# A fused transformer layer: f32 scores, in-PSUM exponentials and DMA transposes instead of split f16 scores and PE transposes

## What is computed

```python
q = (x @ Wq).reshape(B, N, HEADS, DIM_HEAD).transpose(0, 2, 1, 3)      # x: layernorm of x
k = (context @ Wk).reshape(B, M, HEADS, DIM_HEAD).transpose(0, 2, 1, 3)
v = (context @ Wv).reshape(B, M, HEADS, DIM_HEAD).transpose(0, 2, 1, 3)
dots = jnp.einsum('bhnd,bhmd->bhnm', q, k) * SCALE
attn = jax.nn.softmax(dots, axis=-1)
out = jnp.einsum('bhnm,bhmd->bhnd', attn, v)
out = out.transpose(0, 2, 1, 3).reshape(B, N, HEADS * DIM_HEAD)
return out @ Wo + bo
```

## Time and profile before

| | |
|---|---|
| median of 3 runs | 1029.28 us (1024.49 to 1030.27) |
| the profiled execution's own time | 1028.92 us |
| its span, first to last instruction | 1027.0 us |
| PE, DVE, POOL, ACT busy | 870.6, 831.1, 774.3, 684.0 us |
| PE weight loads (PEld, beside PE) | 720.6 us |
| mean granted TensorE clock | 0.935 of full speed |

### The profile page before, as it was taken

How to read it: one execution, slowest core, us unless ns; L and a number is a source line. 1 busy time by engine, 2 the same in 40 slices (tenths; PEclk the granted TensorE clock), 3 DMA queues, 4 the chain that set the end, 5 groups by cost and what they waited for, 6 DMA issues and landing times.

```text
span 1027.0 us, 29818 instructions
## 1 busy us (share of the span) xinstructions
PE 870.6 (85%) x8554; PEld 720.6 (70%) x8554; DVE 831.1 (81%) x2343; ACT 684.0 (67%) x2029; POOL 774.3 (75%) x1237
## 2 busy tenths in 40 slices
PE   7989998999999999999999999999998461049895
PEld 7777786878787887878787887887776261036664
DVE  5899888989999989899999999998988657025563
ACT  3777776778777778778777777777775113037774
POOL 5788888898989898888889898989886503735554
PEclk9999999999999999999999999999999655559998
DMA  9111111111111111111111211111100840111120
GB/s 233 33 33 33 32 33 33 33 33 36 49 42 32 31 31 31 31 31 31 31 31 32 59 33 31 31 31 31 31 2 2 129 162 14 52 43 53 47 54 17
DMA packets 56836, 45.11 MB, mean 44 GB/s; under 512 B 8367, under 2 KB 54578, under 8 KB 56769
## 3 DMA queue, kind: packets, MB, share of 16 engines
q1 hardware_dynamic: 54464, 40.01, 15.9%
q0 software_dynamic: 2304, 4.25, 1.3%
HBM read 37.25 MB, written 7.52 MB: 44 GB/s over the span
## 4 chain that ended last, share of the span: by engine, by line
PE 36%; POOL 31%; issue 13%; DVE 12%; ACT 4%; DMA 1%; POOLq 1%; DVEq 1%; ACTq 0%; SPq 0%
POOL Pn L925 10%; PE bank L396 6%; PE bank L373 6%; PE bank L420 4%; POOL cT L916 4%; PE bank L1369 3%; PE bank L413 3%; PE bank L385 3%; POOL sorted_rows L1232 3%; POOL chi L906 2%; PE bank L1384 2%; DVE cs L839 2%; DVE nmax L783 2%; POOL clo L910 2%; DVE Tl L777 1%
## 5 line engine op out<-in xcount | busy, mean ns | idle before, releaser
L925 POOL TENSOR_TENSOR Pn<-Pe,rsum 128x1028 f32<-128x1028 f32 x128 | 243.1, 1899 | 74.4 <-DVE rsum L798 74.4
L713 ACT ACTIVATE Pe<-bank,nmax 128x257 f32<-128x257 f32 x512 | 240.5, 475 | 30.1 <-DVE nmax L783 29.5
L783 DVE TENSOR_REDUCE nmax<-bank 128x1 f32<-128x257 f32 x512 | 202.0, 415 | 35.3 <-PE bank L373 34.0
L373 PE MATMUL bank<-cT,qh 96*128 96x257 f16 x1024 | 184.8, 275 | 21.1 <-ACT Pe L713 19.6
L777 DVE TENSOR_TENSOR Tl<-bank,Th 128x512 f16<-128x512 f32 x256 | 173.8, 680 | 0.5 <-ACT Th L702 0.4
L702 ACT ACTIVATE Th<-bank 128x512 f16<-128x512 f32 x256 | 141.3, 595 | 48.5 <-PE bank L420 48.5
L420 PE MATMUL bank<-identf,Pn 128*128 128x128 f32 x1024 | 149.3, 274 | 0.0
L373 PE MATMUL bank<-cT,ql 96*128 96x257 f16 x512 | 139.2, 272 | 0.0
L420 PEld LDWEIGHTS bank<-identf,Pn 128*128 128x128 f32 x1024 | 115.1, 142 | 6.1
L373 PEld LDWEIGHTS bank<-cT,qh 96*128 96x128 f16 x1024 | 90.3, 97 | 38.3 <-issue 15.9
L713 ACT ACTIVATION_READ_ACCUMULATOR Pe<-bank,nmax 128x1 f32 x512 | 103.8, 203 | 0.0
(11 more groups left out here) (213 smaller groups left out, 2444.4 us busy)
## 6 DMA issues: line engine op xcount, KB each, us to landing
rawT<-in_dram SPq DMA_DIRECT2D x32, 385.5 KB, 3.9
raw<-in_dram SPq DMA_DIRECT2D x32, 384.0 KB, 4.4
sorted_rows<-fill SPq DMA_DIRECT2D x1, 2620.0 KB, 21.1
xs<-sorted_rows SPq DMA_DIRECT2D x40, 65.5 KB, 1.8
R<-in_dram SPq DMA_DIRECT2D x4, 512.0 KB, 5.9
Z<-last_rows SPq DMA_DIRECT2D x128, 2.2 KB
w1r<-in_dram SPq DMA_DIRECT2D x4, 512.0 KB, 13.7
w2fr<-in_dram SPq DMA_DIRECT2D x4, 512.0 KB, 14.2
```

The source lines that it names most:

```text
L373: last = nc.tensor.matmul(bank[SB[t]][:, 0:M], w[:, par, b, t * P:(t + 1) * P], cT[:, s4, c, 0:M], start=(k == 0), stop=(k == 2))
L713: nc.scalar.activation(Pe[:, n_par(j + 1), t, :], bank[SB[t]][:, 0:M], ACT.Exp, bias=nmax[:, n_par(j + 1), t:t + 1], accum_out=sums[:, n_p ...
L783: nc.vector.tensor_reduce(nmax[:, n_par(j + 1), t:t + 1], bank[SB[t]][:, 0:M], AX.X, ALU.max, negate=True).then_inc(s_nmax, 1)
L925: nc.gpsimd.tensor_tensor(Pn[:, par, :, :], Pe[:, par, :, :], rsum[:, par, :].unsqueeze(2).broadcast_to([P, QT, M]), ALU.mult)\
```

## The change

- The scores are one f32 matmul for each tile, out of f32 queries `qf` and the context as it was loaded, `rawT`. The halves `cT`, `qh` and `ql` are gone, on ACT, POOL and DVE.
- The four tiles of scores have a PSUM bank each (`quad`). ACT writes the exponentials over the scores; then it makes the high halves of the probabilities (`PHL[..., 0, :]`, f16), scaled by the reciprocal sums; DVE makes the low halves (`PHL[..., 1, :]`, semaphore `s_Pl`) in one instruction for each tile. The product on POOL is gone. Scores of n+1 in bank t wait for the low half of n from it.
- One DMA transpose for each sequence turns both halves, 512 KB, from `PHL` into `PT`. It is issued by SP and signals `s_T`; `pe_probsT`, `Th` and `Tl` are gone. ACT waits for the transpose of n-1 before it writes the high halves of n+1 in the same buffer.
- SP runs the steps as well. The context of group g+2 is loaded in the step jj = 0 of group g, and waits for the last scores of group g (`s_S`), since `rawT` is now read by PE itself; `Z` is loaded in the step jj = 1.
- A group's output is summed over its four steps in PSUM, with one residual add for each group; `pe_pv` comes last in PE's step.

```diff
-        def pe_scores(n, par, b, s4, tiles):
-            wait(nc.tensor, s_cTh, n + 1)
-            wait(nc.tensor, s_cT, n + 1)
-            for t in tiles:
-                wait(nc.tensor, s_exp, QT * n + 1 if t == 3 else QT * (n - 1) + (t or 3) + 1)
-                for k, (w, c) in enumerate(((qh, 0), (qh, 1), (ql, 0))):
-                    last = nc.tensor.matmul(bank[SB[t]][:, 0:M], w[:, par, b, t * P:(t + 1) * P],
-                                            cT[:, s4, c, 0:M], start=(k == 0), stop=(k == 2))
-                last.then_inc(s_S, 1)
+        def pe_scores(n, gpar, b, turns):
+            wait(nc.tensor, s_ctxT[gpar], 16 * turns)
+            for t in range(QT):
+                wait(nc.tensor, s_Pl, QT * (n - 1) + t + 1)
+                nc.tensor.matmul(bank[t][:, 0:M], qf[:, gpar, b, t * P:(t + 1) * P], rawT[:, gpar, b, :],
+                                 start=True, stop=True).then_inc(s_S, 1)
...
+            wait(nc.tensor, s_T[par], 16 * turns)
...
-        def pe_probsT(n, par, c):
-            wait(nc.tensor, s_Tl, MC * (n - 1) + c + 1)
-            for t in range(QT):
-                last = nc.tensor.transpose(bank[4 + c][:, t * P:(t + 1) * P], Pn[:, par, t, c * P:(c + 1) * P],
-                                           identf[:, :])
-            last.then_inc(s_T, 1)
...
             n, g, jj, gp = where(it, j)
             if exists(n + 1):
                 if (j + 1) % GB == 0:
-                    wait(nc.tensor, s_ql, n + 5)
-                pe_scores(n + 1, ((j + 1) // GB) % NP2, (j + 1) % GB, (j + 1) % 4, (0, 1, 2))
+                    wait(nc.tensor, s_qf, n + 5)
+                pe_scores(n + 1, ((j + 1) // GB) % NP2, (j + 1) % GB, it + 1 + (j + 1) // NC8)
+            if exists(n):
+                pe_mix_free(it, j)
+                wait(nc.tensor, s_elo, n + 1)
+                wait(nc.tensor, s_L12, n)
+                nc.tensor.transpose(bankh[6][:, 1024 - P:1024], e12p[:, n_par(j), :], ident[:, :]).then_inc(s_left, 1)
             if exists(n + 5):
-                pe_mix_free(it, j)
                 pe_q(n + 5, (j + 1) % GB, bass.ds(P * (g + 1 + (jj + 1) // GB), P))
-            if exists(n + 1):
-                pe_scores(n + 1, ((j + 1) // GB) % NP2, (j + 1) % GB, (j + 1) % 4, (3,))
+            if exists(n - 6):
+                if jj == 2:
+                    wait(nc.tensor, s_Ol, GB * g)
+                pe_y(n, (jj + 2) % GB, gp if jj < 2 else 1 - gp, g - 1)
             if exists(n - 1):
                 pe_pv(n - 1, (j - 1) % NP2, (j - 1) % NC8, ((j - 1) // GB) % NP2, (j - 1) % GB,
-                      it + 1 + (j - 1) // NC8)
-            if exists(n - 5):
-                if jj == 1:
-                    wait(nc.tensor, s_Ol, GB * g)
-                wait(nc.tensor, s_L12, n if n_static(n) is None else min(n, B))
-                pe_y(n, (jj + 3) % GB, gp if jj == 0 else 1 - gp)
+                      it + 1 + (j - 1) // NC8, 4 * it + (j - 1) // 2 + 1)
             if exists(n):
-                wait(nc.tensor, s_elo, n + 1)
-                wait(nc.tensor, s_L12, n)
-                nc.tensor.transpose(bankh[7][:, 0:P], e12p[:, n_par(j), :], ident[:, :]).then_inc(s_left, 1)
-                wait(nc.tensor, s_pn, n + 1)
-                pe_probsT(n, n_par(j), 0)
...
         def act_step(it, j):
             n, g, jj, gp = where(it, j)
-            if exists(n - 1):
-                wait(nc.scalar, s_PV, n - 2)
-                for c in range(MC):
-                    wait(nc.scalar, s_T, MC * (n - 1) + c + 1)
-                    nc.scalar.activation(Th[:, n_par(j - 1), c, :], bank[4 + c][:, :], ACT.Copy).then_inc(s_Th, 1)
-            for t in range(QT):
-                if t == 2 and exists(n + 4):
-                    if (j + 4) % GB == 0:
-                        wait(nc.scalar, s_ctxT[((j + 4) // GB) % NP2],
-                             16 * (it + 1 + ((j + 4) // GB - ((j + 4) // GB) % NP2) // NP2))
-                    act_cT(n + 4, (j + 4) % 4, ((j + 4) // GB) % NP2, (j + 4) % GB)
-                if exists(n + 1):
-                    if t == 0:
-                        wait(nc.scalar, s_elo, n)
+            if exists(n + 1):
+                p = n_par(j + 1)
+                for t in range(QT):
                     wait(nc.scalar, s_nmax, QT * (n + 1) + t + 1)
-                    nc.scalar.activation(Pe[:, n_par(j + 1), t, :], bank[SB[t]][:, 0:M], ACT.Exp,
-                                         bias=nmax[:, n_par(j + 1), t:t + 1],
-                                         accum_out=sums[:, n_par(j + 1), t:t + 1]).then_inc(s_exp, 1)
-                if t == 2 and exists(n + 5):
-                    act_q(n + 5, (gp + 1 + (jj + 1) // GB) % NP2, (j + 1) % GB)
+                    nc.scalar.activation(bank[t][:, 0:M], bank[t][:, 0:M], ACT.Exp, bias=nmax[:, p, t:t + 1],
+                                         accum_out=sums[:, p, t:t + 1]).then_inc(s_exp, 1)
+                wait(nc.scalar, s_T[p], 16 * (4 * it + (j + 1) // 2))
+                for t in range(QT):
+                    if t % 2 == 0:
+                        wait(nc.scalar, s_rs, 2 * (n + 1) + t // 2 + 1)
+                    nc.scalar.activation(PHL[:, p, t, 0, :], bank[t][:, 0:MK], ACT.Identity, scale=rsum[:, p, t:t + 1])\
+                        .then_inc(s_Ph, 1)
+            if exists(n + 5):
+                act_q(n + 5, (gp + 1 + (jj + 1) // GB) % NP2, (j + 1) % GB)
...
         def dve_step(it, j):
             n, g, jj, gp = where(it, j)
-            for kind, t in (("max", 0), ("max", 1), ("low", 0), ("max", 2), ("low", 1), ("max", 3)):
-                if kind == "low" and exists(n - 1):
-                    wait(nc.vector, s_Th, MC * (n - 1) + t + 1)
-                    nc.vector.tensor_tensor(Tl[:, n_par(j - 1), t, :], bank[4 + t][:, :], Th[:, n_par(j - 1), t, :],
-                                            ALU.subtract).then_inc(s_Tl, 1)
-                if t == 3:
+            p = n_par(j + 1)
+            for t in range(QT):
+                if exists(n + 1):
+                    wait(nc.vector, s_S, QT * (n + 1) + t + 1)
+                    nc.vector.tensor_reduce(nmax[:, p, t:t + 1], bank[t][:, 0:M], AX.X, ALU.max, negate=True)\
+                        .then_inc(s_nmax, 1)
+                if t == 1:
                     dve_stat_waits(it, j, n, g, jj)
-                if kind == "max" and exists(n + 1):
-                    wait(nc.vector, s_S, QT * (n + 1) + t + 1)
-                    nc.vector.tensor_reduce(nmax[:, n_par(j + 1), t:t + 1], bank[SB[t]][:, 0:M], AX.X, ALU.max,
-                                            negate=True).then_inc(s_nmax, 1)
             dve_stat(it, j, g, jj, gp)
+            if exists(n):
+                wait(nc.vector, s_PV, n - 1)
+                wait(nc.vector, s_left, n + 1)
+                nc.vector.tensor_copy(L12[:, n_par(j), :], bankh[6][:, 1024 - P:1024]).then_inc(s_L12, 1)
+            if exists(n + 1):
+                wait(nc.vector, s_ehi, n)
+                dve_recip(n + 1, p, 0)
+            if jj == 2 and exists(g - 2, G):
+                wait(nc.vector, s_m["stat"], g - 1)
+            if exists(n - 2):
+                wait(nc.vector, s_Oh, n - 1)
+                sl = (slice(None), ((j - 2) // GB) % NP2, slice(None), slice(((j - 2) % GB) * N, ((j - 2) % GB + 1) * N))
+                nc.vector.tensor_tensor(Ol[sl], bank[5][0:CC, :].rearrange("p (h t) -> p h t", h=H), Oh[sl],
+                                        ALU.subtract).then_inc(s_Ol, 1)
+            if jj == 2 and exists(g - 2, G):
+                nc.vector.bn_aggr(mv[:, gp, :], stats2[:, gp, :]).then_inc(s_m["mv"], 1)
+            if exists(n + 1):
+                dve_recip(n + 1, p, 1)
             dve_mix_a(it, j)
-            if jj == 1 and exists(g - 2, G):
-                wait(nc.vector, s_m["stat"], g - 1)
-            if exists(n + 5):
-                dve_q(n + 5, (gp + 1 + (jj + 1) // GB) % NP2, (j + 1) % GB)
-            if jj == 1 and exists(g - 2, G):
-                nc.vector.bn_aggr(mv[:, gp, :], stats2[:, gp, :]).then_inc(s_m["mv"], 1)
+            if exists(n + 1):
+                wait(nc.vector, s_elo, n)
+                for t in range(QT):
+                    if t % 2 == 0:
+                        wait(nc.vector, s_Ph, QT * (n + 1) + t + 2)
+                        nc.vector.tensor_tensor(p4[:, p, t:t + 2], quad[:, t:t + 2, MK], rsum[:, p, t:t + 2],
+                                                ALU.mult).then_inc(s_p4, 1)
+                    nc.vector.scalar_tensor_tensor(PHL[:, p, t, 1, :], bank[t][:, 0:MK], rsum[:, p, t:t + 1],
+                                                   PHL[:, p, t, 0, :], ALU.mult, ALU.subtract).then_inc(s_Pl, 1)
...
             def load_ctx(g, par):
                 b0 = GB * g
-                wait(sp, s_clo, GB * (g - 1))
-                wait(sp, s_cT, GB * (g - 1))
+                if not isinstance(g, int) or g >= 2:
+                    wait(sp, s_clo, GB * (g - 1))
```

(35 more changed lines are left out.)

229 lines of the change are left out of this document (83 added, 146 removed).

## The result

The changed kernel takes 1276.53 us (median of 4 runs, 1273.21 to 1280.07), beside 1027.14 us (1024.49 to 1030.27, 4 runs) for the kernel before on the same chip: a ratio of 1.243 [1.237, 1.248]. It is slower by 249 us. Each experiment has runs of the kernel before beside it, at 1026 to 1030 us; so kernels are compared by their ratios to it, and a difference of ratios is turned into us with 1027.

The account below looks back on a forecast made before the run. PE, DVE and POOL were taken as close to bound together. Plain steps -10 us plus 30 × (5.8 stall + 1.5 clock) gave +209 on 1028.9, so 1238 us; 8 in 10 within 1115 to 1400.

Parts of the forecast that it names:

- The stall behind the loads, with its clock: SP's queue: transpose of jj = 1 waits behind the loads; 5.8 us stall plus 1.5 us clock, in 30 groups.
- X: SP's queue: time for a transpose's 512 KB behind the loads; 1.6 to 6.1 us, middle 3.8 taken.
- its 4.0 us of stall: SP's queue: stall by the skill page's 261 GB/s, with X 2.0 us and the sum below 1184.
- The clock: TensorE: falls to 1.2 GHz after every stall; 1.5 us a group, ends 0 and 3.
- The plain step: A step without other stalls: latencies from maxima to low halves add up; 5.9 us against 5.98, -10 us over 128.
- POOL as relieved: POOL: loses `Pn`, 1.90 us per step, and the low half of `cT`, so no longer near the bound.
- 5.9 us three times and 13 once: Starts of steps: expected spacing in us if the main case holds, one step in four stalled.
- the queue doesn't hold the transpose back: Rival, SP's queue: transpose packets run among the loads'; stall 2.4 us, 1091 us in all; 8%.
- Faster: Rival, plain step: the chain overlaps better, steps take 5.45 us, -68 us, 961 us in all; 5%.
- The transposes are the bound: Rival, SP's queue: from X = 8 transposes pace the pipeline, 1397 us; 1947 at X = 12.3; 11%.

Follow-up runs that it names:

- experiment 2: Changed kernel with POOL's `e12p` block moved ahead of the time mix: 1207.71 us, ratio 1.178.
- 3: Changed kernel with both moves, context loads issued in jj = 2 instead of jj = 0 and `e12p` ahead of the time mix: 988.11 us, ratio 0.963.
- experiment 1: Changed kernel with the context loads and their wait moved from SP's step jj = 0 to jj = 2: 1071.58 us, ratio 1.044.
- experiment 5: Changed kernel with PE's 12 query matmuls made nine times over in steps jj = 2, to keep TensorE's clock up: 1286.38 us, ratio 1.249.
- 6: Kernel of experiment 5 with the `Z` loads moved from jj = 1 to jj = 3: 1250.55 us, ratio 1.212.
- 7: Changed kernel with only the `Z` loads moved from jj = 1 to jj = 3: 1279.21 us, ratio 1.241.
- experiments 9 to 11: Against the kernel with both moves: one f32 score matmul per step made twice, 1016.47 us; one maximum made twice, 1030.29; time mix reordered on DVE, 985.04.
- e12p: POOL's two instructions of 0.20 us on the probabilities of key 257; moved ahead of the time mix in the changed kernel: 1207.71 us, ratio 1.178.
- experiment 8: Kernel with both moves, every transpose issued twice, the second into a spare buffer, both waited for: 1116.73 us, ratio 1.084.
- experiment 11: Kernel with both moves, the rest of DVE's time mix moved from behind the low halves to ahead of them: 985.04 us, ratio 0.956.

## Why the prediction was right, and where it was not

The forecast was 1238 us and the measured time lies 3% above it, inside the range, and the term that decides was there for the reason given. That the total is so near is in part luck: the plain step came out 28 us better than the sum had it, and a stall of 67 us was not in it. The sum had three terms, and the runs measured each.

- **The stall behind the loads, with its clock: 30 × (5.8 + 1.5) = 219 predicted, 221 us measured** (experiment 2 against 3; 204 for experiment 1 against the changed kernel). ACT waits 5.98 us in the timeline, 169.6 us in 31 times in all. But the 5.8 came out right by two errors of 2 us that cancel. The first is X, the time that the transpose adds behind the loads' data. Worked out from the packets in the trace, as medians of the 30 stalls, the loads' data end 4.3 us after `rawT` is issued (4.4 in the working), the transpose's last packet follows 1.8 us later (X = 3.8 there), and it lands 0.5 after that (0.5 there): 6.7 us, 6.85 in the stall shown, where the working gave 8.7. And ACT wants it 0.9 us after that issue, where the working gave 2.9: it set the end of the last scores 0.8 us ahead of the next first maximum, but PE's four scores run from 513.12 to 515.02 and DVE's maxima from 513.77, 1.25 us ahead of that end. Four scores and four maxima overlap; they don't stand one behind the other.
- The Trainium skill, page "DMA: Bandwidth & Descriptors", section on latency and other measured facts, has a DMA transpose with a non-contiguous middle dimension at 261 GB/s. An estimate from that figure is 2.0 us for 512 KB. Behind the loads, where X is taken, the trace agrees: 1.8 us, and 277 GB/s in the window at 520.00; with the DMA engines to itself the transpose takes 2.5 us at about 218 GB/s. So of the prediction's two values for X the page's was right and the middle taken was not, and yet its 4.0 us of stall was further off than 5.8: that working, too, has ACT want the transpose 2 us later than it does, and there no other error cancels this.
- **The clock: 1.5 us predicted, 1.2 to 1.4 us on the step of the stall** (experiment 5). That the compute engines could use what it gives back was taken for granted; they can't, as long as the next transpose stands behind `Z` (experiments 5, 6 and 7).
- **The plain step: 5.9 predicted, 5.57 measured** without either stall (over all 127 steps 5.69, beside 5.98 before); -38 us in place of -10. Six of the eight steps take 5.1 to 5.5 us, steps 0 and 1 take 5.91 and 6.53. The added latencies were right in kind (experiments 9 to 11: the chain through DVE sets the step), but the step is 0.3 us shorter than their sum. It was not the prices: the f32 score held (eight records in 1.90 us, 0.43 a tile), the low halves were underpriced, 0.39 from start to start where 0.36 was taken, and ACT's high halves, 0.36 for 0.33. It was the time mix, of which the working let nearly all, 1.3 us, stand behind the low halves (4.60 to 5.9). In experiment 3 the last low half ends 5.06 us after the first maximum, and the next step's first maximum starts 0.50 us later (means of the same 80 steps); most of the mix's work lies elsewhere, ahead of the low halves. One step, in DVE's timeline:

```profile
504.31 1.73 DVE L729 TENSOR_REDUCE nmax<-quad 128x1 f32<-128x257 f32 x4
...
508.46 0.87 DVE L760 SCALAR_TENSOR_TENSOR PHL<-quad,rsum,PHL 128x256 f16<-128x256 f32 x2
509.25 0.56 DVE L795 TENSOR_TENSOR_SCAN cs<-onesn,fab 128x32 f32<-128x32 f32 x4
509.73 1.63 DVE L729 TENSOR_REDUCE nmax<-quad 128x1 f32<-128x257 f32 x4
```

- **Missed: the order on POOL, 67 us.** The prediction dismissed POOL as relieved, looked at its sum of work alone, and never asked what its instructions now stand behind. The move of `e12p` is in the change; what is queued behind it, PE's transpose at the head of its step and DVE's copy, was to be read from the order, and `rec` behind the low halves too. It is one step in eight, 10.05 us long instead of 5.14.

With the plain step 28 us better, the stall 2 worse and the missing term of 67, the sum goes from +209 to +250. Of the sign "5.9 us three times and 13 once" the 13 held (12.98 and 12.67); the others are 5.4 to 6.5, with the 10.05 among them.

The rivals: *the queue doesn't hold the transpose back* would have given a landing 5.3 us after `rawT`'s issue; it was 6.85, and the packets show the transpose's behind the loads'. Why its issue takes 3.90 us there and not 2.0 is not shown. *Faster* was wrong for the change as it stands, though its premise, plain steps of 5.45, was nearly right: it fails only by the two orders. *The transposes are the bound* is out by experiments 3 and 8: only twice as many come near it. The Trainium skill, page "VectorE: DVE Perf Modes", section on the three transpose paths, gives 1309 ns for a block of 128x128. An estimate from it, if the sixteen blocks paid that one by one, is 20.9 us; in the trace all sixteen land 4.5 us after the start of the issue (median), so here it is not a price for each block.

What stays open: whether SP's slow issue behind the loads costs anything beyond the loads' data, what bounds experiment 8, and why in experiment 11 step 0 loses nearly what step 1 gains.

## What to carry to other kernels

When a transfer becomes part of the chain of each step, read the issuing queue as an engine in program order: a prefetch that waits for something late must not stand ahead of a transfer that is wanted soon, and here its place alone was worth 204 to 221 us of 1277, a sixth of the time. Ask the same of an engine that is relieved: its small outputs may now stand behind waits that its old work had covered, and its busy share doesn't show it. When a cost is removed and nothing comes back, look for the wait that took its place before calling the cost unreal.
